# One phase for the first mixture of experts and the front of the state-space layer

## What is computed

```python
x = x + linear_attention(layernorm(x))     # layer 1: 8 heads of 64, decaying state
x = x + mixture(layernorm(x))              # layer 2
x = x + state_space(layernorm(x))          # layer 3
x = x + routed(layernorm(x))               # layer 4: mixture with capacity, plus a shared expert

def mixture(t):                            # 4096 tokens, 8 experts, the best 2 of each token
    topv, topi = top_k(t @ router_w.T, 2); w = softmax(topv)
    return sum over the two choices k:  w[k] * gelu(t @ w1[topi[k]].T) @ w2[topi[k]].T     # 128 -> 256 -> 128

def state_space(t):
    u = rmsnorm(t) * norm_w @ Win + b_in               # 128 -> 256 channels
    v = causal_conv(u, conv_w, 4 taps) + conv_b        # per channel, along the sequence
    h[s] = h[s-1] @ A[channel] + v[s] * B[channel]     # 16 states per channel
    return (h . C[channel]) @ Wout + b_out + t
```

## Time and profile before

| engine | busy us | share of the span | instructions |
|---|---|---|---|
| PE | 860.1 | 85% | 9276 |
| DVE | 554.6 | 55% | 1617 |
| POOL | 474.5 | 47% | 501 |
| ACT | 449.2 | 45% | 957 |

### The profile page before, as it was taken

One profiled execution on the slowest core, in us unless ns is written; L12 is line 12 of the kernel. 1 busy time (PEld: TensorE's weight loads), 2 busy tenths in 40 slices (PEclk: granted clock), 3 DMA queues, 4 the chain that ended last, 5 costly groups with the idle time before them and its releaser, 6 DMA issues. The chain is left out here.

```text
span 1006.1 us, 25740 instructions
## 1 busy us (share of the span) xinstructions
PE 860.1 (85%) x9276; PEld 721.8 (72%) x9276; DVE 554.6 (55%) x1617; ACT 449.2 (45%) x957; POOL 474.5 (47%) x501
## 2 busy tenths in 40 slices
PE   4999999999998518989567789999967999999990
PEld 1777777777776516877555579999966679999990
DVE  4666666676576534656359776455467713222225
ACT  5545455354453104555146757333504444444443
POOL 3235353343444463777666100126422376767764
PEclk9999999999999757999779999999998999999995
DMA  7676800000000013333330010000023023322245
GB/s 237 236 283 260 332 21 11 13 16 5 21 10 14 22 43 86 109 103 99 80 96 2 3 24 2 3 4 1 1 80 133 24 70 83 86 85 90 82 116 167
DMA packets 72920, 79.31 MB, mean 79 GB/s; under 512 B 14429, under 2 KB 56676, under 8 KB 72320
## 3 DMA queue, kind: packets, MB, share of 16 engines
q1 hardware_dynamic: 61744, 59.69, 18.8%
q0 software_dynamic: 9216, 16.84, 4.9%
q10 hardware_dynamic: 1872, 1.58, 0.5%
HBM read 32.46 MB, written 47.77 MB: 80 GB/s over the span
## 5 line engine op out<-in xcount | busy, mean ns | idle before, releaser
L436 POOL TENSOR_TENSOR attn_qd<-attn_qT,attn_qpow 128x512 f32<-128x512 f32 x32 | 51.3, 1604 | 129.9 <-DVE attn_qT L727 129.9
L1466 ACT ACTIVATE routed_hT<-routed_hid,routed_B 128x256 f32<-128x256 f32 x160 | 65.7, 470 | 81.1 <-PE routed_hid L1389 81.1
L1035 POOL DMA_INDIRECT mixed<-moe_outs,moe_target x80 | 77.7, 972 | 39.2 <-DVE moe_outs L1137 16.7
L1307 POOL DMA_INDIRECT results<-routed_outs,routed_target x80 | 78.5, 981 | 30.0 <-issue 16.3
L1292 POOL DMA_INDIRECT queue_in<-routed_XN,routed_slot x64 | 63.1, 985 | 46.4 <-DVE routed_slot L1567 22.2
L1401 PE MATMUL routed_outp<-routed_W,routed_hT 128*128 128x128 f32 x640 | 77.8, 275 | 0.0
L1389 PE MATMUL routed_hid<-routed_cols,routed_W 128*128 128x256 f32 x320 | 75.8, 380 | 0.5 <-DVE routed_cols L1615 0.5
L1401 PEld LDWEIGHTS routed_outp<-routed_W,routed_hT 128*128 128x128 f32 x640 | 74.7, 192 | 0.1
L426 POOL DMA_INDIRECT sorted_rows<-attn_sent_rows,attn_slot x56 | 57.1, 1019 | 18.3 <-issue 14.1
L1389 PEld LDWEIGHTS routed_hid<-routed_cols,routed_W 128*128 128x128 f32 x320 | 57.8, 191 | 6.8 <-ACT routed_shared L1445 0.7
L307 ACT ACTIVATE attn_kd<-attn_turn,attn_kpow 128x256 f32<-128x256 f32 x56 | 23.5, 470 | 77.3 <-PE attn_turn L585 77.3
(11 more groups left out here) (332 smaller groups left out, 2270.6 us busy)
## 6 DMA issues: line engine op xcount, KB each, us to landing
sorted_rows<-attn_vacant SPq DMA_DIRECT2D x8, 2080.0 KB, 8.7
moe_rows<-sorted_rows SPq DMA_DIRECT2D x44, 130.0 KB
queue_in<-attn_empty SPq DMA_DIRECT2D x8, 645.0 KB, 6.6
routed_rows<-queue_in SPq DMA_DIRECT2D x40, 129.0 KB, 2.3
results<-attn_zero SPq DMA_DIRECT2D x8, 512.0 KB, 8.1
ssm_turn_buf<-mixed SPq DMA_DIRECT2D x16, 256.0 KB, 3.7
routed_W<-m1w SPq DMA_DIRECT2D x2, 2048.0 KB, 10.2
xs<-x SPq DMA_DIRECT2D x8, 256.0 KB, 4.4
```

What stands on the lines that cost most here:

```text
L436: pool.tensor_tensor(wide(of_pair(qd, p)), wide(of_pair(qT, p)), qpow[:, p * P:(p + 1) * P].unsqueeze(1).to_broadcast([P, BATCH, P]), ALU. ...
L1035: pool.indirect_dma_start(results, bass.IndirectOffsetOnAxis(target[:, n:n + 1], 0), outs[q][:, j * P:(j + 1) * P], None, bounds_check=2 * ...
L1307: pool.indirect_dma_start(results, bass.IndirectOffsetOnAxis(target[:, n:n + 1], 0), outs[t % KEPT_BACK][:, j * P:(j + 1) * P], None, boun ...
L1466: last = act.activation(hT[t % 2][:, m * GROUP:(m + 1) * GROUP], banks[q % 4][:, (m % 2) * GROUP:(m % 2 + 1) * GROUP], ACT.Silu, bias=B1[: ...
```

## The change

The mixture phase and the state-space phase become one (`mixed_space_phase`), without a loop and without a meeting of the engines between them.

1. The blocks are ordered by chunk first and expert second, so that the results of chunk c are complete after `complete(c)` = 4c + 11 blocks. There are 39 blocks. The running count of each expert is kept per chunk (`place` grows to nine sets), and the table is worked out with one block per partition.
2. All engines go through `TICKS` = 53 ticks. Tick t holds the work of block t (until 38), one square (until t = 39), and the steps of a chunk's front at fixed ticks: chunk c has its results added at tick 15 + 4c (POOL) and 16 + 4c (DVE), statistics at 16 + 4c, shift and norm at 17 + 4c, the turn at 18 + 4c, the products at 19 + 4c and 20 + 4c, and the taps at 22 + 4c to 24 + 4c.
3. A square uses one pair of PSUM banks instead of five banks in turn, and both copies are ACT's; the next square waits for both. The turned rows of a block have one bank instead of two. The turned chunk and the product share one bank.
4. Of the two additions of results, POOL keeps the first and DVE takes the second.

```diff
-BLOCKS = 2 * BATCH * SEQ // GROUP + EXPERTS
+BLOCKS = (2 * BATCH * SEQ + EXPERTS * (GROUP - 1)) // GROUP
+def complete(c):
+    return (2 * WIDE * (c + 1) + EXPERTS * (GROUP - 1)) // GROUP
...
+            front.normalize(dve, xs, 0, 0)
+            grids()                          # 10 small operations that fill constant tiles
             dve.wait_ge(s["decays"], 3)
...
             shifts(LAST)
+            blocks_of(slice(0, LAST))        # compare and reduce, 128 x 896
             logits_read(LAST, proj[1])
...
+        turn, outp = pb[0][:, 0:GROUP], (pb[1][:, 0:GROUP], pb[4][:, 0:GROUP])
+        hid, tokens_at, inputs_at, squares_b, squares_c = pb[2:4], pb[5], pb[5], pb[6], pb[7]
+        PERIOD = complete(1) - complete(0)
+        def due(t, begin):
+            c, part = divmod(t - begin, PERIOD)
+            return c if part == 0 and 0 <= c < CHUNKS else None
+        FETCHED_BACK, MIXED, STATED, SCALED, TURNED, INPUT, KEPT_IN, CONVOLVED = 18, 15, 16, 17, 18, 19, 20, 22
+        TICKS = CONVOLVED + 2 + PERIOD * (CHUNKS - 1) + 1
...
+            def fetch_back(c):               # SP
+                sp.wait_ge(s["sent"], BODY + complete(c))
...
+            for n in range(TICKS):           # SP
+                if n < BLOCKS:
+                    fetch(n)
+                if due(n, FETCHED_BACK) is not None:
+                    fetch_back(due(n, FETCHED_BACK))
...
+            for t in range(TICKS):           # POOL
+                if t < BLOCKS:
+                    sent_back(t)
+                if 2 <= t < BLOCKS + 2:
+                    landed(t - 2)
...
+                if due(t, STATED) is not None:
+                    deviations(due(t, STATED))
+                if due(t, MIXED) is not None:
+                    mixed(due(t, MIXED))
...
+            def squares(m):                  # PE
+                if m:
+                    pe.wait_ge(s["lev_b"], m)
+                    pe.wait_ge(s["lev_c"], m)
...
+            for t in range(TICKS):           # PE
+                if t + 2 < BLOCKS:
+                    rows_turned(t + 2)
+                if t + 1 < BLOCKS:
+                    hidden_of(t + 1)
+                if t < BLOCKS:
+                    output_of(t)
+                if due(t, INPUT + 1) is not None:
+                    input_product(due(t, INPUT + 1), 1)
+                if due(t, INPUT) is not None:
+                    input_product(due(t, INPUT), 0)
+                if due(t, TURNED) is not None:
+                    columns(due(t, TURNED))
+                if t < NSQUARES:
+                    squares(t)
...
+            for t in range(TICKS):           # ACT
+                if t < BLOCKS:
+                    gelu_of(t)
+                if t + 2 < BLOCKS:
+                    first_weights(t + 2)
+                if due(t, INPUT) is not None:
+                    columns(due(t, INPUT))
+                for h in range(2):
+                    if due(t, KEPT_IN + h) is not None:
+                        channels(due(t, KEPT_IN + h), h)
+                        last_tap(due(t, KEPT_IN + h), h)
+                if due(t, SCALED) is not None:
+                    tokens(due(t, SCALED), 0)
+                    tokens(due(t, SCALED), 1)
+                if 1 <= t <= NSQUARES:
+                    power_kept(t - 1)        # both copies of square t - 1
...
+            for t in range(TICKS):           # DVE
+                if t + 2 < BLOCKS:
+                    columns_of(t + 2)
+                if t < BLOCKS:
+                    kept_of(t)               # waits for output_of(t)
+                if t + 2 < BLOCKS:
+                    second_weights(t + 2)
+                if due(t, STATED) is not None:
+                    mixed(due(t, STATED))
+                    stated(due(t, STATED))
+                if due(t, SCALED) is not None:
+                    scaled_means(due(t, SCALED))
+                for n in range(TAPS - 1):
+                    if due(t, CONVOLVED + n) is not None:
+                        convolved(due(t, CONVOLVED + n), n)
```

More of the change, by code:

```diff
@@ L961, in _ @@
[L961 to L966, removed]
@@ L972, in _ @@
[L972 to L975, removed]
+            dve.wait_ge(s["put"], at(LAST, PLACED, PLACED))
+            blocks_of(slice(LAST, CHUNKS))
+            tabled(dve.tensor_tensor(fresh[:, :], blocks[:, EXPERTS:], blocks[:, 0:SPANS], ALU.subtract))
@@ L1722, in first_vectors, with mixed_space_phase @@
             pool.tensor_copy(row[:, :, 0:1], table[:, :, STATES:STATES + 1])
-def state_space_phase(nc, xs, of, powers, scratch, sorting, results):
+def mixed_space_phase(nc, xs, of, W1, W2, table, sorted_rows, powers, scratch, results):
     with ExitStack() as ctx:
@@ L1801, in _, with fetch @@
         def _(sp):
-            for c in range(CHUNKS):
+            def fetch(n):
+                first = sp.value_load(table.first_row[n:n + 1, 0:1], min_val=0, max_val=EXPERTS * REGION)
+                sp.wait_ge(s["rows_read"], n + 1)
+                sp.dma_start(by_row(rows[n % BODY]), sorted_rows[bass.ds(first, GROUP), :].rearrange("(p j) f -> p j f", p=P)
+                             ).then_inc(fetched[n % BODY], 16)
+            def fetch_back(c):
+                sp.wait_ge(s["sent"], BODY + complete(c))
                 if c >= 2:
@@ L1827, in mixed @@
                 chunk = slice(c * WIDE, (c + 1) * WIDE)
-                for k in range(2):
-                    if k:
-                        pool.wait_ge(s["added"], 2 * c + 1)
-                    pool.tensor_tensor(xs[:, chunk], xs[:, chunk], back[k][:, chunk], ALU.add).then_inc(s["added"], 1)
+                pool.tensor_tensor(xs[:, chunk], xs[:, chunk], back[0][:, chunk], ALU.add).then_inc(s["added"], 1)
             def deviations(c):
@@ new lines, in _, with rows_turned, hidden_of @@
+            pe.sem_inc(s["outp"], 2)
+            def rows_turned(n):
+                pe.wait_ge(fetched[n % BODY], 16 * (n // BODY + 1))
+                pe.wait_ge(s["cols"], n + 2)
+                for j in range(2):
+                    mm = pe.transpose(turn[:, j * P:(j + 1) * P], rows[n % BODY][:, j * TAGGED:j * TAGGED + D], ident[:, :])
+                mm.then_inc(s["turned"], 1)
+            def hidden_of(n):
+                pe.wait_ge(s["w1_in"], n + 1)
+                pe.wait_ge(s["cols"], n + 3)
+                pe.wait_ge(s["act"], n + 1)
+                for m in range(HB):
+                    mm = pe.matmul(hid[n % 2][:, m * GROUP:(m + 1) * GROUP], w1[n % 2][:, m * P:(m + 1) * P], cols[n % 2],
+                                   start=True, stop=True)
+                mm.then_inc(s["hid"], 1)
```

438 lines of the change are left out of this document (175 added, 263 removed).

## The result

Slower: four executions of the changed kernel took 1016.03 to 1022.04 us, median **1019.49 us**, against 1006.75 for four of the kernel before: a ratio of 1.0127 with a 95% interval of 1.0101 to 1.0153. The profiled execution is the slowest of the four (1022.04 us, span 1020.2). In it PE is busy for 867.4 us, DVE for 540.7, POOL for 462.6 and ACT for 453.2.

What follows compares the result with a forecast made beforehand. POOL was taken to bound the mixture, a five-engine chain the front. Terms of 194.8, clock 13.2 and wider squares 2 made 210 against 205.0 us; 1006.1 + 5.0 + 1.6 = 1012.7 us, range 994 to 1030.

Steps and rivals of the forecast that it cites:

- the tick of a block and a square: Ticks 0 to 15: PE bounds, block 1.97 plus square 0.93 make 2.90 us a tick, 46.4 us in all.
- 10.3 plus 2.2 for the clock: PE's squares, blocks, turn and product after each group's wait, up to the next output, plus 2.2 us lost at half clock.
- the 113: Ticks 16 to 35: five groups of 20.4 us, 102 in all, with 2.2 each for the clock, 113 us.
- the wider squares: Squares of later levels, 80 columns instead of 65, add at most 0.2 us each, an estimated 2 in all.
- All behind it is unchanged: From the first transposes behind the front onward, nothing changes in time.
- The stall: Each group: PE's square waits about 6 us for ACT's copies, queued behind the norm that waits for DVE's shift.
- The tail: From tick 36 to the transposes, the last chunks' chain takes 46.4 us, or 48.6 with 2.2 for the clock.
- The clock: PE falls to half clock after each of six waits, losing 2.2 us each (from 1.8 to 4.6), 13.2 in all.
- The clock holds: Rival, faster: with waits a little shorter or the clock staying, the 13.2 us go: 999.5 us, chance 0.17.
- The overlap works: Rival, faster: the norm does not hold up the copies, groups cost 14.3 instead of 20.4 us: 969 us, chance 0.14.
- Long half-clock stretches: Rival, slower: each return of PE takes 9.2 us at half clock, losing 4.6 instead of 2.2: 1027 us, chance 0.11.
- DVE and POOL get in each other's way: Rival, slower: second addition and third taps slowed, 2.5 us more a group, 15 in six: 1028 us, chance 0.10.

Runs made afterwards that it cites:

- experiments 5 and 6: Changed kernel with the first 16 squares computed twice, then instead with the two halves of a square apart in the first 16 ticks: 1035.18 and 1023.48 us.
- experiment 3: Changed kernel with 21 idle PE products where PE waits for ACT's copies, in six ticks: 1006.36 us, ratio 0.9997.
- experiment 7: Changed kernel with POOL's half of the result addition one tick earlier (14 instead of 15): 1015.91 us, ratio 1.0088.
- experiment 1: Changed kernel with ACT's two copies of the last square ahead of the front's ACT work in every tick: 999.26 us, ratio 0.9921.
- experiment 4: Changed kernel with DVE's shift one tick later, ACT's norm two, what follows two or three, ACT's copies ahead of taps and norm: 972.75 us, ratio 0.9642.
- experiment 8: Kernel of experiment 4 with all stages of the seventh chunk one tick and of the eighth two ticks closer: 973.02 us.

## Why the prediction was right in direction and short in size

It said 5.0 us more on the span; the profiled spans differ by 14.1, the medians by 12.7.

- **The step that failed** is the tick of a block and a square, "2.90 ... So PE bounds these ticks: 16 x 2.90 = 46.4". PE does bound them, but at 3.20: I added the price of a block among blocks and that of a square among squares, and the change puts them in turn. Two changes of shape a tick cost 0.30 (experiments 5 and 6), 4.9 us in 16 ticks. The same is missing in the groups. PE's part from the end of the wait to the next output, which I put at 10.3 plus 2.2 for the clock, took 13.5 in the fourth group (519.87 to 533.36, below), and 10.9 to 11.3 in the groups of experiment 3, where the clock stays at 1.00: 0.6 to 1.0 more than my 10.3 with no clock in it. The groups took 3.9 more than the 113, of which the wider squares account for some 1 (a square went from 1.08 us to 1.25) and the clock for 0.5. So to the 7.1 us by which the stretch was missed the changes of shape give the 4.9, and by these figures about 2.5 in the groups, where no run sets them apart; the other errors are tenths and nearly cancel.

```profile
519.87 1.22 PE L1824 MATMUL ssm_pb<-powers_XB,powers_XC 64*64 64x72 f32 x16 [5.47 <-ACT powers_XC L2057]
533.36 1.02 PE L1841 MATMUL ssm_pb<-ssm_hT,powers_WIN 128*128 128x512 f32 x2
```

- **"All behind it is unchanged"** failed by 1.3 in the profiled execution: the stretch hands over PE at half clock, and the first transposes pay (9.14 for 7.61). It is not so in every one: in that of experiment 7, whose last products are at half clock too (2.04), they took 7.59.
- **The stall** was right in place and cause. The chain from an output to the held square was put at 10.1 us; it took 10.3, 9.5, 10.8, 9.8 and 9.9, in part by errors that cancel (the last rival below). The tail was right as well (48.9 for 48.6).
- **The clock** was right in sum: 6 x 2.2 = 13.2 predicted, 13.1 to 13.6 measured by filling the wait. The 2.2 was a choice between 1.8 and 4.6 whose reason no run tests. The rival "The clock holds" compared the wait with the 5.3 us of idleness of the earlier trace rows, for most of which the clock had held; that comparison decides nothing here, as in experiment 1 the clock fell with waits of 1.45 and 3.03.
- **The rivals.** "The overlap works" had about the right price (groups of 14.3 and 969 us; 15.0 to 15.7 and 972.75 in experiment 4), but its condition does not hold in this kernel: the norm does hold up the copies. "Long half-clock stretches": half clock lasted 6.0 us in the first group (the window from 452 to 458 has 0.60, so up to 456.8), not 9.2. "DVE and POOL get in each other's way": I looked for it at the taps, which took 1.41 in the groups; it was at the head of the chain, in a cast that I had priced at 0.17, and was worth 4.7 us of the stretch (experiment 7). It did not lengthen the chain beyond my sum, because other terms were put too high. In the first group POOL's two powers took 2.1 us, for up to 3.0, the norm 1.65 for 1.76, the two copies 0.65 for 0.8. That the chain came out at 10.1 is thus partly luck.

Open: why the start of the stretch differs by up to 10 us from one profiled execution to another, why the transposes return at full speed in some and not in others, what in a change of shape takes the 0.15 us, and what sets the last chunk's end in experiment 8.

## What to carry to other kernels

When two phases are merged by writing an order for each engine, look on every engine for the instruction that waits longest and ask what stands behind it: moving ACT's copies ahead, and a norm and what follows it two to three ticks back, turned 13 us lost into 33 won, with not one operation changed. Price an operation by a row in which its neighbours are those that it will have, since PE's products of two shapes in turn cost more here than both apart (3.20 us a tick for 2.90). PE paid twice for idling here, once for the wait (35.1 us in six) and once for the clock on its return (13); idle products in the wait show how much is which.

## What the runs showed of the hardware that I had not expected

- A change between 128x128 and 64x64 products cost PE 0.15 to 0.17 us, with no idle time in the profile.
- One product in fp32 was two records of 0.114 us (40 products of 128x128 by 128: 80 records, 9.10 us).
- A 128x2 cast on DVE lasted until POOL's addition of 128x512 ended, 0.92 to 1.08 us and once 1.91, against 0.15 to 0.17 otherwise.
- With PE kept busy by useless work at full clock the kernel was 13 us faster than with PE idle.
